# Recurrence of a gated layer: gates handled one by one, candidate and new state by scans over pairs, activation scale from a register

## The chip, the cores and the metric

The kernel runs on one core of a Trainium2 chip. The metric is the device time of one execution in microseconds (us), taken as the median over runs. In the text: PE is TensorE (matmuls; PEld its weight loads), DVE is VectorE, ACT is ScalarE, POOL is GpSimd. L12 is line 12 of the kernel's file.

## What is computed

A sandwich of two blocks on x of shape (8, 512, 128): attention in a neighbourhood of 13 tokens, then a mixture of experts whose routing comes from a recurrent layer. Each block is followed by a layer norm and a residual. The part that matters here is the recurrence, 512 steps over the sequence with a batch of 8 and a state of 1024 = 8 chunks x 128:

```python
def step(h, xw_t):
    hw = h @ gru_w_hh.T
    xr, xz, xn = jnp.split(xw_t, 3, axis=-1)
    hr, hz, hnn = jnp.split(hw, 3, axis=-1)
    r = jax.nn.sigmoid(xr + hr)
    z = jax.nn.sigmoid(xz + hz)
    n = jnp.tanh(xn + r * hnn)
    h_new = (1.0 - z) * n + z * h
    return (h_new, h_new)
_, hs = jax.lax.scan(step, h0, jnp.swapaxes(xw, 0, 1))
```

## The kernel before

The program is a row of blocks: loading and transposing weights, attention, preparing the recurrence, the recurrence, loading expert weights, routing scores and experts. The change touches the block that prepares the recurrence (from L760) and the recurrence itself (from L831). Both are written out by hand for each engine, with semaphores; nothing is scheduled by a tool, and each engine runs its list in order.

The state lies transposed: 128 partitions, and in the free dimension 8 chunks x 8 batch entries. It is cut into two halves, A and B, of 4 chunks, 32 elements for each partition. `h_parts` holds the state as two float16 parts (rounded value and remainder), which are the stationary operand of the matmuls; `h_full` holds it in float32. The steps run in pairs (q = 0 and 1), and 8 pairs make a tile of 16 steps; there are 32 tiles.

In each step PE computes the gates of both halves, in one PSUM bank each: 64 matmuls for A and 64 for B (`state_share`, L868). A's sum needs state half B as well, and the other way round. So PE waits for the new half A (`h_ready[0]`, L905), does the 32 matmuls of bank A that use it and 16 of bank B, waits for the new half B (`h_ready[1]`, L911), does the other 32 of bank A, signals `gates_ps[0]`, does the last 48 of bank B, and signals `gates_ps[1]`. Eight matmuls each of the token's share (L876) stand in between.

DVE handles first half A wholly, then half B (L979 to L984), each with three functions:

- `turn`: two transposes from PSUM to `turned`, gates r and z together (128x256, L946), then the candidate's share (128x128, L947), which frees the bank.
- `before_tanh`: adds the two float16 parts' products (L928, once for r and z, once for the candidate), waits for ACT's sigmoid over r and z (L1012, 128x64, result `rz`), multiplies r by the candidate's share (L957) and adds the token's share `xn_pair` (L959).
- `after_tanh`: waits for ACT's tanh (L1015) and for POOL, then L968 (`fresh` = tanh x (1-z)), L970 (the sum with `keep` = z x h as the first float16 part), L971 (the same sum in float32), L973 (the remainder, which sets `h_ready`).

POOL makes `keep` (L855) and `not_z` (L856) out of z. ACT gives both activations their scale as a [128, 1] operand (`scale=unscale[:, 0:1]`), and copies the new state to `history` (L1020, semaphore `kept`). After half B DVE does a share of the routing dot products (L746 and L751 for q = 0; L934, L937, L742 and L751 for q = 1). At the first pair of each tile PE, ACT and DVE also turn the tile before into routing rows (L724, L728, L733, L736).

## Time and profile before

| what | value |
|---|---|
| time, median of 3 runs | 4774.18 us (4764.96 to 4792.71) |
| profiled execution, span | 4784.5 us |
| PE, DVE, ACT, POOL busy | 83%, 69%, 25%, 16% of the span |
| recurrence | from about 577 us to about 4330 us of the span (first and last sigmoid of L1012) |
| granted TensorE clock in the recurrence | 0.99 to 1.00 of full speed |

For the profiled execution no time is given other than its span, the time from the first to the last instruction; it lies between the runs' lowest and highest time. In a timeline a row has the start, the length, the engine, the line and the operation, and in brackets how long the engine had been idle and what ended that. Rows of instructions of one line that follow each other are merged (x2, x80). VectorE starts an instruction that waits for nothing before the one ahead has ended, so the difference of two starts is what the first one costs the row.

### The profile page before, as it was taken

To read this page: it belongs to the slowest core of one execution; us is meant where nothing else is said; L and a number is where in the kernel's file an instruction comes from. 1 tells how busy PE (TensorE), PEld (TensorE's weight loads), DVE (VectorE), ACT (ScalarE), POOL (GpSimd) and SP (SyncE) were. 2 spreads that over 40 slices of the span, in tenths; PEclk is the share of its full clock that TensorE was granted. 3 is DMA by queue.
4 is the path that set the end of the run, shared out by engine and by line. 5 is a ranking of instruction groups with operands and counts; after the bars stand their busy time and mean duration, and the time that the engine had idled before them with its cause. 6 is when DMAs were issued, how large, how long until landed. Compare 5 with 4: busy or idle time off the path is not lost. (4 is left out here: it accounts for less than half of the span.)

```text
span 4784.5 us, 185112 instructions
## 1 busy us (share of the span) xinstructions
PE 3953.2 (83%) x76430; PEld 2476.3 (52%) x76430; DVE 3284.3 (69%) x13296; ACT 1204.3 (25%) x3094; POOL 768.7 (16%) x2439
## 2 busy tenths in 40 slices
PE   4998488888888888888888888888888888885999
PEld 3776354555544545544545545555554555453665
DVE  2668577777777777777777777777777777776555
ACT  1111322222222222222222222222222222222232
POOL 1111011111111111111111111111111111110000
PEclk9869799999999999999999999999999999997999
DMA  2001300000000000000000000000000000001000
GB/s 59 18 31 57 111 0 0 0 0 0 0 0 0 0 0 0 0 0 0 0 0 0 0 0 0 0 0 0 0 0 0 0 0 0 0 0 32 9 13 11
DMA packets 45745, 40.85 MB, mean 9 GB/s; under 512 B 11668, under 2 KB 39572, under 8 KB 45716
## 3 DMA queue, kind: packets, MB, share of 16 engines
q1 hardware_dynamic: 45716, 40.48, 2.7%
q8 instruction: 16, 0.26, 0.0%
q14 instruction: 13, 0.11, 0.0%
HBM read 36.28 MB, written 4.19 MB: 8 GB/s over the span
## 5 line engine op out<-in xcount | busy, mean ns | idle before, releaser
L868 PE MATMUL psum<-room,h_parts 128*32 128x384 f16 x65536 | 2904.9, 328 | 595.1 <-DVE h_parts L973 595.1
L868 PEld LDWEIGHTS psum<-room,h_parts 128*32 128x32 f16 x65536 | 1670.9, 97 | 1695.4 <-DVE h_parts L973 912.2
L1012 ACT ACTIVATE rz<-gates,unscale 128x64 f32<-128x64 f32 x1024 | 356.3, 348 | 1830.3 <-DVE gates L928 1830.3
L855 POOL TENSOR_TENSOR keep<-rz,h_full 128x32 f32<-128x32 f32 x1024 | 262.3, 256 | 2991.5 <-ACT rz L1012 2984.8
L946 DVE STREAM_TRANSPOSE turned<-psum 128x256 f32<-128x256 f32 x1024 | 454.1, 443 | 51.8 <-PE psum L868 16.9
L968 DVE TENSOR_TENSOR fresh<-n_act,not_z 128x32 f32<-128x32 f32 x1024 | 196.6, 192 | 401.7 <-ACT n_act L1015 397.4
L1015 ACT ACTIVATE n_act<-pre_n,unscale 128x32 f32<-128x32 f32 x1024 | 329.5, 322 | 497.4 <-DVE pre_n L959 497.4
L957 DVE TENSOR_TENSOR pre_n<-rz,gates 128x32 f32<-128x32 f32 x1024 | 197.2, 193 | 301.8 <-ACT rz L1012 301.8
L751 DVE TENSOR_REDUCE gram<-products 128x640 f32 (+3 forms) x528 | 327.6, 620 | 109.2 <-DVE products L742 53.8
L856 POOL TENSOR_SCALAR not_z<-rz,neg_h_scale,h_scale 128x32 f32<-128x32 f32 x1024 | 375.1, 366 | 0.0
L876 PE MATMUL psum<-w_ih_s,x_now 128*32 128x256 f16 x6152 | 305.1, 275 | 44.9 <-DVE turned L947 35.7
L928 DVE TENSOR_TENSOR gates<-turned 128x64 f32<-128x64 f32 (+1 forms) x2048 | 309.6, 187 | 0.0
L1291 PE MATMUL psum<-xn2T,room 128*128 x576 | 262.0, 600 | 38.8 <-DVE room L1366 31.4
L746 DVE TENSOR_TENSOR products<-routes 128x640 f32 (+1 forms) x264 | 218.0, 826 | 101.2 <-ACT routes L736 100.6
L947 DVE STREAM_TRANSPOSE turned<-psum 128x128 f32<-128x128 f32 x1024 | 280.1, 274 | 0.0
L1020 ACT COPY history<-h_parts 128x128 f16 (+1 forms) x512 | 152.6, 298 | 459.8 <-DVE h_parts L973 459.8
L876 PEld LDWEIGHTS psum<-w_ih_s,x_now 128*32 128x32 f16 x6152 | 160.0, 98 | 162.1 <-DVE turned L947 48.1
L959 DVE TENSOR_TENSOR pre_n<-pre_n,xn_pair 128x32 f32<-128x32 f32 x1024 | 196.7, 192 | 34.9
L973 DVE TENSOR_TENSOR h_parts<-h_full,h_parts 128x32 f16<-128x32 f32 x1024 | 196.2, 192 | 35.6
L970 DVE TENSOR_TENSOR h_parts<-fresh,keep 128x32 f16<-128x32 f32 x1024 | 196.5, 192 | 34.9
L1366 DVE TENSOR_TENSOR room<-room,psum 128x512 f32<-128x512 f32 x144 | 98.1, 686 | 142.9 <-ACT room L1308 140.9
L971 DVE TENSOR_TENSOR h_full<-fresh,keep 128x32 f32<-128x32 f32 x1024 | 188.4, 184 | 0.0
(151 smaller groups left out, 2725.6 us busy)
## 6 DMA issues: line engine op xcount, KB each, us to landing
xs_room<-in_L_ffn_gru_w_hh_dram SPq DMA_DIRECT2D x16, 1536.0 KB, 6.2
room<-in_L_attn_x_dram SPq DMA_DIRECT2D x8, 256.0 KB, 5.4
x_scratch<-room SPq DMA_DIRECT2D x8, 256.0 KB, 2.3
room<-x_scratch SPq DMA_DIRECT2D x32, 64.0 KB, 2.2
out_dram<-room SPq DMA_DIRECT2D x32, 64.0 KB, 2.0
xs_room<-in_L_ffn_gru_w_ih_dram SPq DMA_DIRECT2D x3, 512.0 KB, 5.1
xs_room<-in_L_ffn_gate_w_dram SPq DMA_DIRECT2D x2, 512.0 KB, 4.6
xs_room<-in_L_ffn_up_w_dram SPq DMA_DIRECT2D x2, 512.0 KB, 3.9
```

The costliest lines, as they stand in the source:

```text
L746: return nc.vector.tensor_tensor(products[:, :, :], routes[:, 0, bass.ds(e, 1), :].to_broadcast([P, NSHIFT, P]), routes[:, 0, bass.ds(e, N ...
L751: return nc.vector.tensor_reduce(dst, products[:, 0:n, :], axis=AX_X, op=ALU.add)
L855: nc.gpsimd.tensor_tensor(keep[:, half, :], rz[:, half, 1, :], h_full[:, q, half * HB:(half + 1) * HB], ALU.mult)
L856: nc.gpsimd.tensor_scalar(not_z[:, half, :], rz[:, half, 1, :], neg_h_scale[:, 0:1], h_scale_f[:, 0:1], ALU.mult, ALU.add).then_inc(keep_d ...
L868: last = nc.tensor.matmul(psum[32 * j:32 * j + 32, half, 0:3 * P], h_parts[:, q, c, :], w_hh_s[:, s, half, 4 * c + j, :, :].rearrange("p g ...
L876: last = nc.tensor.matmul(psum[32 * j:32 * j + 32, columns, 0:2 * P], x_now[:, :], w_ih_s[:, s, j, place:place + 2, :].rearrange("p g r -> ...
L928: return nc.vector.tensor_tensor(by_chunk(gates[:, half, g:g + n, :].rearrange("p g k -> p (g k)")), by_part[:, :, 2 * q, :], by_part[:, : ...
L946: nc.vector.transpose(turned[:, half, 0:2, :], bank[:, 0:2, :]).then_inc(rz_turned[half], 1)
L947: nc.vector.transpose(turned[:, half, 2:3, :], bank[:, 2:3, :]).then_inc(bank_free[half], 1)
L1012: nc.scalar.activation(rz[:, half, :, :], gates[:, half, 0:2, :], ACT.Sigmoid, scale=unscale[:, 0:1]).then_inc(rz_done[half], 1)
L1015: nc.scalar.activation(n_act[:, half, :], pre_n[:, half, 1, :], ACT.Tanh, scale=unscale[:, 0:1]).then_inc(n_done[half], 1)
L1291: last = nc.tensor.matmul(psum[:, 2 * (u % RING) + k, :], expT[:, e, FC * k + f, :], toks, start=True, stop=True)
```

## The change

It rewrites what DVE, ACT and POOL do in a step, and leaves PE's list as it is.

- r, z and the candidate's share are transposed and summed one by one (`to_gates`): three transposes of 128x128 and three sums of 128x32, where two transposes and two sums stood. ACT has a sigmoid for r and one for z, each of 128x32.
- The product and sum ahead of the tanh become one scan (`tensor_tensor_scan` with multiply and add) over 64 elements in which pairs stand side by side: `r_pairs` = (0, r) and `hx_pairs` = (candidate's share, token's share). The scan's running value at the first element of a pair is 0 x old + share, and at the second r x share + token's share. The new state comes from a second scan over `z_pairs` = (0, not_z) and `nk_pairs` = (tanh, keep). The results are read from every second element.
- The state in float32 lies in `h_pairs`, at every second element. Its first float16 part is a copy of it (L977) instead of a sum of its own.
- `not_z` moves from POOL to DVE; POOL keeps the product z x h.
- ACT takes the scale from a register that is loaded once ahead of the loops, and the function table for sigmoid is loaded there too.
- DVE's wait for `kept` moves from the transposes of half A to its second scan.
- POOL clears `r_pairs` and `z_pairs` in the preparing block.

```diff
@@ -664,18 +664,17 @@
         h_parts = sb("h_parts", [P, 2, CH, 4 * B], F16)
         x_now = sb("x_now", [P, 4 * B], F16)
-        h_full = sb("h_full", [P, 2, CH * B])
+        h_pairs = sb("h_pairs", [P, 2, CH * B, 2])
         turned = sb("turned", [P, 2, 3, P])
-        gates = sb("gates", [P, 2, 3, HB])
+        gates = sb("gates", [P, 2, 2, HB])
         xn_turned = sb("xn_turned", [P, 2 * P])
-        xn_pair = sb("xn_pair", [P, CH, 2, B])
+        hx_pairs = sb("hx_pairs", [P, 2, CH * B, 2])
         neg_h_scale = sb("neg_h_scale", [P, 1])
-        rz = sb("rz", [P, 2, 2, HB])
-        pre_n = sb("pre_n", [P, 2, 2, HB])
-        n_act = sb("n_act", [P, 2, HB])
-        keep = sb("keep", [P, 2, HB])
-        not_z = sb("not_z", [P, 2, HB])
-        fresh = sb("fresh", [P, 2, HB])
+        r_pairs = sb("r_pairs", [P, 2, HB, 2])
+        z_act = sb("z_act", [P, 2, HB])
+        pre_n = sb("pre_n", [P, 2, HB, 2])
+        z_pairs = sb("z_pairs", [P, 2, HB, 2])
+        nk_pairs = sb("nk_pairs", [P, 2, HB, 2])
         x_mean = sb("x_mean", [P, B])
         history = sb("history", [P, CH, 2, SP_T, B], F16)
         ident_16 = sb("ident_16", [P, P], F16)
...
@@ -765,6 +765,8 @@
                 nc.gpsimd.memset(x_parts[:, L, :], 0.0)
                 nc.gpsimd.memset(history[:, :, :, :, :], 0.0)
                 nc.gpsimd.memset(x_tile[:, :], 0.0)
+                nc.gpsimd.memset(r_pairs[:, :, :, :], 0.0)
+                nc.gpsimd.memset(z_pairs[:, :, :, :], 0.0)
                 nc.gpsimd.tensor_copy(ident_16[:, :], ident[:, :])
                 pool.wait_ge(h0_top, 1)
                 nc.gpsimd.partition_all_reduce(h_all[:, :], w_top[:, :], P, RMAX).then_inc(h0_all, 1)
...
@@ -851,9 +854,9 @@
                     nc.gpsimd.tensor_copy(x_now[:, :].rearrange("p (t k) -> p t k", t=2), x_parts[:, bass.ds(t0 + 2, 2), :]).then_inc(x_staged, 1)
                     for q in range(2):
                         for half in range(2):
-                            pool.wait_ge(rz_done[half], t0 + q + 1)
-                            nc.gpsimd.tensor_tensor(keep[:, half, :], rz[:, half, 1, :], h_full[:, q, half * HB:(half + 1) * HB], ALU.mult)
-                            nc.gpsimd.tensor_scalar(not_z[:, half, :], rz[:, half, 1, :], neg_h_scale[:, 0:1], h_scale_f[:, 0:1], ALU.mult, ALU.add).then_inc(keep_done[half], 1)
+                            pool.wait_ge(z_done[half], t0 + q + 1)
+                            nc.gpsimd.tensor_tensor(nk_pairs[:, half, :, 1], z_act[:, half, :], h_pairs[:, q, half * HB:(half + 1) * HB, 1],
+                                                    ALU.mult).then_inc(keep_done[half], 1)
                     if first:
                         nc.gpsimd.tensor_copy(x_tile[:, :], xn2T[:, bass.ds(n * P, P)]).then_inc(tile_staged, 1)
@@ -922,11 +925,9 @@
             @block.vector
             def _(dve):
-                def summed(q, half, g, n):
-                    by_part = turned[:, half, g:g + n, :].rearrange("p g (k s b) -> p (g k) s b", s=4, b=B)
-                    return nc.vector.tensor_tensor(by_chunk(gates[:, half, g:g + n, :].rearrange("p g k -> p (g k)")),
-                                                   by_part[:, :, 2 * q, :], by_part[:, :, 2 * q + 1, :], ALU.add)
+                def summed(q, half, g, dst):
+                    by_part = turned[:, half, g, :].rearrange("p (k s b) -> p k s b", s=4, b=B)
+                    return nc.vector.tensor_tensor(by_chunk(dst), by_part[:, :, 2 * q, :], by_part[:, :, 2 * q + 1, :], ALU.add)
                 def turn_xn(pairs):
@@ -934,41 +935,46 @@
                     nc.vector.transpose(xn_turned[:, :], psum[:, XN_BANK, 0:2 * P]).then_inc(xn_read, 1)
                     dve.wait_ge(xn_read, pairs)
                     by_part = xn_turned[:, :].rearrange("p (k q s b) -> p k q s b", q=2, s=2, b=B)
-                    nc.vector.tensor_tensor(xn_pair[:, :, :, :], by_part[:, :, :, 0, :], by_part[:, :, :, 1, :],
-                                            ALU.add).then_inc(xn_ready, 1)
-                def turn(t1, q, half):
+                    nc.vector.tensor_tensor(hx_pairs[:, :, :, 1].rearrange("p q (c b) -> p c q b", b=B),
+                                            by_part[:, :, :, 0, :], by_part[:, :, :, 1, :], ALU.add).then_inc(xn_ready, 1)
+                def to_gates(t1, q, half):
                     bank = psum[:, half, 0:3 * P].rearrange("p (g r) -> p g r", g=3)
                     dve.wait_ge(gates_ps[half], t1)
+                    nc.vector.transpose(turned[:, half, 0, :], bank[:, 0, :]).then_inc(r_turned[half], 1)
+                    nc.vector.transpose(turned[:, half, 1, :], bank[:, 1, :]).then_inc(z_turned[half], 1)
+                    dve.wait_ge(r_turned[half], t1)
+                    summed(q, half, 0, gates[:, half, 0, :]).then_inc(r_in[half], 1)
+                    nc.vector.transpose(turned[:, half, 2, :], bank[:, 2, :]).then_inc(bank_free[half], 1)
+                    dve.wait_ge(z_turned[half], t1)
+                    summed(q, half, 1, gates[:, half, 1, :]).then_inc(z_in[half], 1)
+                    dve.wait_ge(bank_free[half], t1 + 1)
+                    summed(q, half, 2, hx_pairs[:, q, half * HB:(half + 1) * HB, 0]).then_inc(n_in[half], 1)
+                def row(pairs):
+                    return pairs.rearrange("p k two -> p (k two)")
+                def to_state(t1, q, half):
+                    here = slice(half * HB, (half + 1) * HB)
+                    dve.wait_ge(n_in[half], t1)
+                    dve.wait_ge(r_done[half], t1)
+                    nc.vector.tensor_tensor_scan(row(pre_n[:, half, :, :]), row(r_pairs[:, half, :, :]), row(hx_pairs[:, q, here, :]),
+                                                 0.0, ALU.mult, ALU.add).then_inc(pre_done[half], 1)
+                    dve.wait_ge(z_done[half], t1)
+                    nc.vector.tensor_scalar(z_pairs[:, half, :, 1], z_act[:, half, :], neg_h_scale[:, 0:1], h_scale_f[:, 0:1],
+                                            ALU.mult, ALU.add).then_inc(not_z_done[half], 1)
                     if half == 0:
                         dve.wait_ge(kept, t1)
-                    nc.vector.transpose(turned[:, half, 0:2, :], bank[:, 0:2, :]).then_inc(rz_turned[half], 1)
-                    nc.vector.transpose(turned[:, half, 2:3, :], bank[:, 2:3, :]).then_inc(bank_free[half], 1)
-                def before_tanh(t1, q, half):
-                    dve.wait_ge(rz_turned[half], t1)
-                    summed(q, half, 0, 2).then_inc(gates_in[half], 1)
-                    dve.wait_ge(bank_free[half], t1 + 1)
-                    summed(q, half, 2, 1).then_inc(n_in[half], 1)
-                    dve.wait_ge(rz_done[half], t1)
-                    dve.wait_ge(n_in[half], t1)
-                    nc.vector.tensor_tensor(pre_n[:, half, 0, :], rz[:, half, 0, :], gates[:, half, 2, :], ALU.mult).then_inc(hn_scaled[half], 1)
-                    dve.wait_ge(hn_scaled[half], t1)
-                    nc.vector.tensor_tensor(by_chunk(pre_n[:, half, 1, :]), by_chunk(pre_n[:, half, 0, :]),
-                                            xn_pair[:, half * HALF:(half + 1) * HALF, q, :], ALU.add).then_inc(pre_done[half], 1)
-                def after_tanh(t1, q, half):
+                    parts = h_parts[:, 1 - q, half * HALF:(half + 1) * HALF, :]
+                    full = h_pairs[:, 1 - q, here, 1]
+                    dve.wait_ge(not_z_done[half], t1)
+                    dve.wait_ge(keep_done[half], t1)
                     dve.wait_ge(n_done[half], t1)
-                    dve.wait_ge(keep_done[half], t1)
-                    full = h_full[:, 1 - q, half * HB:(half + 1) * HB]
-                    parts = h_parts[:, 1 - q, half * HALF:(half + 1) * HALF, :]
-                    nc.vector.tensor_tensor(fresh[:, half, :], n_act[:, half, :], not_z[:, half, :], ALU.mult).then_inc(fresh_done[half], 1)
-                    dve.wait_ge(fresh_done[half], t1)
-                    nc.vector.tensor_tensor(part(parts, 2 * (1 - q)), by_chunk(fresh[:, half, :]), by_chunk(keep[:, half, :]), ALU.add)
-                    nc.vector.tensor_tensor(full, fresh[:, half, :], keep[:, half, :], ALU.add).then_inc(first_part[half], 1)
+                    nc.vector.tensor_tensor_scan(row(h_pairs[:, 1 - q, here, :]), row(z_pairs[:, half, :, :]), row(nk_pairs[:, half, :, :]),
+                                                 0.0, ALU.mult, ALU.add).then_inc(full_done[half], 1)
+                    dve.wait_ge(full_done[half], t1)
+                    nc.vector.tensor_copy(part(parts, 2 * (1 - q)), by_chunk(full)).then_inc(first_part[half], 1)
                     dve.wait_ge(first_part[half], t1)
                     nc.vector.tensor_tensor(part(parts, 2 * (1 - q) + 1), by_chunk(full), part(parts, 2 * (1 - q)), ALU.subtract).then_inc(h_ready[half], 1)
@@ -976,12 +982,10 @@
                     t0 = n * SP_T + 2 * i
                     for q in range(2):
                         t1 = t0 + q + 1
-                        turn(t1, q, 0)
-                        before_tanh(t1, q, 0)
-                        after_tanh(t1, q, 0)
-                        turn(t1, q, 1)
-                        before_tanh(t1, q, 1)
-                        after_tanh(t1, q, 1)
+                        to_gates(t1, q, 0)
+                        to_state(t1, q, 0)
+                        to_gates(t1, q, 1)
+                        to_state(t1, q, 1)
                         if q == 0:
@@ -1003,17 +1007,24 @@
             @block.scalar
             def _(act):
+                by_unscale = nc.scalar.alloc_register("by_unscale")
+                nc.scalar.reg_load(by_unscale, unscale[0:1, 0:1].bitcast(U32))
+                nc.scalar.preload_act_table(ACT.Sigmoid)
                 def pair(n, i, first):
                     t0 = n * SP_T + 2 * i
                     for q in range(2):
                         t1 = t0 + q + 1
                         for half in range(2):
-                            act.wait_ge(gates_in[half], t1)
-                            nc.scalar.activation(rz[:, half, :, :], gates[:, half, 0:2, :], ACT.Sigmoid,
-                                                 scale=unscale[:, 0:1]).then_inc(rz_done[half], 1)
+                            act.wait_ge(r_in[half], t1)
+                            nc.scalar.activation(r_pairs[:, half, :, 1], gates[:, half, 0, :], ACT.Sigmoid,
+                                                 scale=by_unscale).then_inc(r_done[half], 1)
+                            act.wait_ge(z_in[half], t1)
+                            nc.scalar.activation(z_act[:, half, :], gates[:, half, 1, :], ACT.Sigmoid,
+                                                 scale=by_unscale).then_inc(z_done[half], 1)
                             act.wait_ge(pre_done[half], t1)
-                            nc.scalar.activation(n_act[:, half, :], pre_n[:, half, 1, :], ACT.Tanh,
-                                                 scale=unscale[:, 0:1]).then_inc(n_done[half], 1)
+                            nc.scalar.activation(nk_pairs[:, half, :, 0], pre_n[:, half, :, 1], ACT.Tanh,
+                                                 scale=by_unscale).then_inc(n_done[half], 1)
                         act.wait_ge(h_ready[1], t1 + 1)
                         act.wait_ge(tile_ps, n + 1)
```

How the lists of instructions move, at two places. DVE, half A of a step at q = 0, before (A and B at a semaphore's end are the halves):

```order
L946 STREAM_TRANSPOSE turned<-psum 128x256 [waits kept,gates_psA]
L947 STREAM_TRANSPOSE turned<-psum 128x128
L928 TENSOR_TENSOR gates<-turned 128x64 [waits rz_turnedA]
L952 REGISTER_ALU
L928 TENSOR_TENSOR gates<-turned 128x32 [waits bank_freeA]
L957 TENSOR_TENSOR pre_n<-rz,gates 128x32 [waits n_inA,rz_doneA]
L959 TENSOR_TENSOR pre_n<-pre_n,xn_pair 128x32 [waits hn_scaledA]
L968 TENSOR_TENSOR fresh<-n_act,not_z 128x32 [waits keep_doneA,n_doneA]
L970 TENSOR_TENSOR h_parts<-fresh,keep 128x4x8 [waits fresh_doneA]
L971 TENSOR_TENSOR h_full<-fresh,keep 128x32
L973 TENSOR_TENSOR h_parts<-h_full,h_parts 128x4x8 [waits first_partA]
```

and after the change:

```order
L945 STREAM_TRANSPOSE turned<-psum 128x128 [waits gates_psA]
L946 STREAM_TRANSPOSE turned<-psum 128x128
L930 TENSOR_TENSOR gates<-turned 128x32 [waits r_turnedA]
L949 STREAM_TRANSPOSE turned<-psum 128x128
L930 TENSOR_TENSOR gates<-turned 128x32 [waits z_turnedA]
L952 REGISTER_ALU
L930 TENSOR_TENSOR hx_pairs<-turned 128x32 [waits bank_freeA]
L962 SCALAR_TENSOR_TENSOR pre_n<-r_pairs,hx_pairs 128x64 [waits r_doneA,n_inA]
L965 TENSOR_SCALAR z_pairs<-z_act,neg_h_scale,h_scale 128x32 [waits z_doneA]
L974 SCALAR_TENSOR_TENSOR h_pairs<-z_pairs,nk_pairs 128x64 [waits keep_doneA,n_doneA,not_z_doneA,kept]
L977 CAST h_parts<-h_pairs 128x4x8 [waits full_doneA]
L979 TENSOR_TENSOR h_parts<-h_pairs,h_parts 128x4x8 [waits first_partA]
```

Ten instructions and a register operation have become eleven and a register operation. The two scans are printed as SCALAR_TENSOR_TENSOR of 128x64; the second one has four waits, `kept` among them, and L965 stands ahead of it.

ACT, the entry to the loops and half A of the first step, before:

```order
L838 UNCONDITIONAL_BRANCH
L838 ISA
L1012 ACT_TABLE_LOAD
L1012 ACTIVATE rz<-gates,unscale 128x64 [waits gates_inA]
L1015 ACTIVATE n_act<-pre_n,unscale 128x32 [waits pre_doneA]
```

and after:

```order
L1011 TENSOR_LOAD unscale
L1012 ACT_TABLE_LOAD
L841 UNCONDITIONAL_BRANCH
L841 ISA
L1020 ACTIVATE r_pairs<-gates 128x32 [waits r_inA]
L1023 ACTIVATE z_act<-gates 128x32 [waits z_inA]
L1026 ACTIVATE nk_pairs<-pre_n 128x32 [waits pre_doneA]
```

The table load stood inside the loop over tiles (the branch at L838 opens it) and now stands ahead of it (L841 opens it); one activation has become two.

## Rows read from the trace of the kernel before

**Rows 1.** The page: busy time and share of the span of each engine.
```profile
PE 3953.2 (83%) x76430; PEld 2476.3 (52%) x76430; DVE 3284.3 (69%) x13296; ACT 1204.3 (25%) x3094; POOL 768.7 (16%) x2439
```

**Rows 2.** Timeline, steady recurrence: start us, length us, engine, line, operation, count, [idle before].
```profile
2403.19 3.43 PE L868 MATMUL psum<-room,h_parts 128*32 128x384 f16 x80 [0.50 <-DVE h_parts L973]
...
2404.84 0.44 DVE L946 STREAM_TRANSPOSE turned<-psum 128x256 f32<-128x256 f32 x1
2405.21 0.28 DVE L947 STREAM_TRANSPOSE turned<-psum 128x128 f32<-128x128 f32 x1
2405.41 0.30 DVE L928 TENSOR_TENSOR gates<-turned 128x64 f32<-128x64 f32 x2
2405.62 0.35 ACT L1012 ACTIVATE rz<-gates,unscale 128x64 f32<-128x64 f32 x1 [2.07 <-DVE gates L928]
2406.00 0.19 DVE L957 TENSOR_TENSOR pre_n<-rz,gates 128x32 f32<-128x32 f32 x1 [0.30 <-ACT rz L1012]
2406.05 0.26 POOL L855 TENSOR_TENSOR keep<-rz,h_full 128x32 f32<-128x32 f32 x1 [3.81 <-ACT rz L1012]
2406.23 0.19 DVE L959 TENSOR_TENSOR pre_n<-pre_n,xn_pair 128x32 f32<-128x32 f32 x1
...
2406.30 0.37 POOL L856 TENSOR_SCALAR not_z<-rz,neg_h_scale,h_scale 128x32 f32<-128x32 f32 x1
...
2406.46 0.32 ACT L1015 ACTIVATE n_act<-pre_n,unscale 128x32 f32<-128x32 f32 x1 [0.49 <-DVE pre_n L959]
2406.81 0.19 DVE L968 TENSOR_TENSOR fresh<-n_act,not_z 128x32 f32<-128x32 f32 x1 [0.39 <-ACT n_act L1015]
2407.04 0.19 DVE L970 TENSOR_TENSOR h_parts<-fresh,keep 128x32 f16<-128x32 f32 x1
...
2407.37 0.19 DVE L973 TENSOR_TENSOR h_parts<-h_full,h_parts 128x32 f16<-128x32 f32 x1
2407.48 0.44 DVE L946 STREAM_TRANSPOSE turned<-psum 128x256 f32<-128x256 f32 x1
...
2407.61 1.48 PE L868 MATMUL psum<-room,h_parts 128*32 128x384 f16 x32 [0.77 <-DVE h_parts L973]
...
2410.24 3.05 PEld L868 LDWEIGHTS psum<-room,h_parts 128*32 128x32 f16 x80 [0.67 <-DVE h_parts L973]
2410.24 3.44 PE L868 MATMUL psum<-room,h_parts 128*32 128x384 f16 x80 [0.28 <-DVE h_parts L973]
...
2419.05 0.44 DVE L946 STREAM_TRANSPOSE turned<-psum 128x256 f32<-128x256 f32 x1
```

**Rows 3.** Timeline around the start of a new tile of 16 steps.
```profile
2453.38 1.28 ACT L1012 ACT_TABLE_LOAD   x1 [0.15 <-issue]
...
2455.57 0.35 ACT L1012 ACTIVATE rz<-gates,unscale 128x64 f32<-128x64 f32 x1 [0.91 <-DVE gates L928]
...
2473.13 0.45 DVE L946 STREAM_TRANSPOSE turned<-psum 128x256 f32<-128x256 f32 x1 [1.14 <-PE psum L868]
```

**Rows 4.** Groups by line and shape, VectorE: count | busy us, mean ns | idle before.
```profile
L937 DVE TENSOR_TENSOR xn_pair<-xn_turned 128x128 f32<-128x128 f32 x257 | 75.2, 293 | 8.8
...
L1142 DVE TENSOR_TENSOR room<-room 128x256 f32<-128x256 f32 x21 | 8.9, 425 | 2.0 <-issue 0.4
L1338 DVE TENSOR_SCALAR room<-room,mv,rstd 128x128 f32<-128x128 f32 x32 | 8.9, 342 | 0.7
...
L393 DVE RECIPROCAL total<-total 128x64 f32<-128x64 f32 x8 | 4.4, 553 | 0.6
...
L1142 DVE TENSOR_TENSOR room<-gram,room 128x256 f32<-128x256 f32 x5 | 3.1, 613 | 0.4
```

**Rows 5.** Groups by line and shape, ScalarE.
```profile
L733 ACT ACTIVATE routes<-psum,h_unscale 128x512 f32<-128x512 f32 x99 | 60.6, 682 | 7.0 <-PE psum L728 7.0
...
L736 ACT COPY routes<-psum 128x512 f32<-128x512 f32 x66 | 35.6, 603 | 0.0
...
L1130 ACT ACTIVATE room<-room 128x32 f32<-128x32 f32 x1 | 0.3, 260 | 15.6 <-DVEq L1207 15.6
```

14 lines of the change are left out of this document (8 added, 6 removed).

## The prediction

> **What bounds the kernel now.** I read the page first. PE is busy for 83% of the span and DVE for 69% [rows 1], so the page alone suggests PE. The page's own chain of waits doesn't help, because it covers only the end of the program. The timeline of the steady recurrence does [rows 2]. Two steps take 2419.05 - 2404.84 = 14.21 us, one step 7.1 us, and 512 steps are some 3640 of the 4784.5 us. Within a step DVE works on half A from the transpose at 2404.84 to that of half B at 2407.48, 2.64 us, then as long on half B. The other 1.8 us are PE's first 32 matmuls with the new half B, up to the next transpose. While DVE is on a half, PE comes to a stop: 0.77 us ahead of the matmuls at 2407.61, 0.67 us by its weight loads ahead of those at 2410.24 (0.28 us by the modelled ends of its matmuls), 0.50 us at 2403.19 [rows 2]. So a step ends by the chain DVE, ACT, DVE, ACT, DVE of two halves, one after the other. Each 0.1 us off a half is 1024 x 0.1 = 102 us off the kernel, as long as PE's stops last.
>
> The half in full, as starts from its first transpose [rows 2]: transpose of r and z 0; transpose of the candidate 0.37; sum of r and z 0.57; ACT's sigmoid 0.78; product 1.16; sum 1.39; tanh 1.62; fresh 1.97; first part 2.20; remainder 2.53; next transpose 2.64. From these come the prices I use. An instruction of 32 elements costs 0.22 us if the next one needs its result (0.19 long and 0.03 to be seen), and 0.11 us if not (two in a row take 0.30, the last of them 0.19). A transpose of 128 elements costs the next one 0.20 us and is 0.28 long. ACT starts 0.21 us after a sum starts; DVE starts 0.03 us after ACT ends, POOL 0.08 us.
>
> **The change, part by part.** *Three transposes and three sums.* Transpose r 0, transpose z 0.20, sum r 0.40, transpose of the candidate 0.51, sum z 0.71. The candidate's sum waits for its transpose (0.51 + 0.28 + 0.03) and starts at 0.82. ACT starts r at 0.61 and has it by about 0.90 even if it is as long as the 0.32 of today's 32-element activation. So ACT no longer ends this wait: DVE's own sums do, and the next instruction can start at 0.82 + 0.22 = 1.04, where the product started at 1.16. One more instruction stands in DVE's row, and 0.12 us are won, because the sigmoid now lies beside DVE's work.
>
> *Elements at every second place.* The candidate's sum now writes so, and the copy and the remainder at the end read so. No row has such a step. At no cost the lower end; for the upper the sum at L1142, which takes 425 ns with its elements side by side and 613 ns where it reads `gram`, whose elements lie 10 apart: 188/256 = 0.73 ns for each element, 0.024 us for 32 [rows 4]. I take the upper end, as its row is the only one, and the price is small: 3 x 0.024 = 0.07 us a half. The scans themselves read and write side by side.
>
> *The scans.* The trace has no scan. Below: 64 elements are in and out in 0.19 us, as a plain instruction of that kind. Above: the reciprocal at L393, whose 64 elements go round for several cycles each, 553 ns [rows 4]. A scan's element needs the one before it through a multiply and an add, so 64 elements are 128 dependent operations, and I take the 128-element sum at L937, 293 ns [rows 4]. Then the first scan costs 0.29 + 0.04 up to the tanh, where product and sum cost 0.46 (1.16 to 1.62): 0.13 us won. The second costs 0.32, and the copy after it 0.22; that replaces fresh 0.22, first part 0.11 and full state 0.22 (1.97 to 2.53, 0.56): 0.02 us won. The Trainium skill (DVE: opcode table, Datapath and trigger behaviour) says of the built-in scan that it runs at half throughput, which is the same two cycles for an element. No run here shows it yet.
>
> *The scale from a register.* ACT's activation from PSUM with a [128, 1] scale takes 682 ns for 512 elements, its copy without one 603 ns [rows 5]: 0.08 us for the operand. Taken off today's 0.32 of the tanh this leaves 0.24 us. A 32-element activation with no such operand stands at 260 ns [rows 5], though with its elements four apart. Ends: no gain at all (a register might be read as late as an operand), and 0.09 us. I take 0.08. The Trainium skill (ScalarE: Activation LUTs, What ACT_TABLE_LOAD costs) gives about 93 ns for each such operand; the sum would be 13 us lower by it.
>
> *z, not_z and keep.* ACT starts z at 0.92, and has it at 1.17. POOL's product starts at 1.25 and is there by 1.55. On DVE not_z stands behind the first scan; it starts at about 1.27 and, with two [128, 1] operands, takes some 0.25: L1338, the same with 128 elements, takes 342 ns, less 96 elements at about 1 ns (425 - 293 ns for 128 more) [rows 4]. It is there by 1.55. Both cost nothing as long as the tanh ends later, which it does at about 1.66. The cover is 0.1 us.
>
> *The table load.* 32 loads of 1.28 us go. The one at 2453.38 ends at 2454.66, and ACT then idles another 0.91 us until DVE's sum releases it at 2455.57 [rows 3]: nothing won. The Trainium skill (ScalarE: Activation LUTs, same section) adds a drain of about 1.38 us to each load. That would end at 2456.04, behind the start that the row shows, so the trace disagrees, and I go by the row. The wait for `kept` is for a copy of 0.3 us made in the step before; it had ended at either place.
>
> **Sum.** A half before 2.64 us. Won 0.12 + 0.13 + 0.02 + 0.08 = 0.35, given back 0.07 (and 0.01 of rounding): 0.27 us. Times 1024 = 276 us. Right after a tile's start PE runs late, and DVE waits 1.14 us for it at 2473.13 [rows 3]. That half's gain is lost in at most 32 tiles, 32 x 0.27 = 9 us; I take half, 4 us. PE's stops are 0.28 us and more, so it stays behind DVE elsewhere. 4784.5 - 272 = 4512 for the profiled execution. That lies 10 us over the median of the runs, so the median becomes **4502 us**.
>
> **The rivals.** *POOL or not_z ends last (20%).* DVE's scan and POOL's product meet at 1.04 to 1.55, and not_z runs against POOL's product. If POOL's product could start only when not_z has ended (1.52 + 0.26 + 0.05), the second scan would start at 1.83 instead of 1.66, 0.17 us late. They may overlap in part, so I price 0.12 us: 1024 x 0.12 = 123 more, 4625 us. Against it: today L959 starts at 2406.23 inside POOL's L855 (2406.05 for 0.26) and is 0.19 long, as L968 is with POOL idle [rows 2]. The Trainium skill (SBUF — State Buffer, Who interferes with whom) has it that a DVE instruction with two inputs from SBUF, or in a 2-port mode as `tensor_scalar` can be, and a POOL one that reads SBUF block each other wholly. L959's row doesn't agree.
>
> *The register is no better than the operand (8%).* [...] 0.08 x 1024 = 82 more, 4584 us.
>
> *A scan as cheap as a plain instruction (12%).* Each is 0.10 us shorter. The first counts in full; the second scan's start then meets POOL's 1.55, so about 0.18 in all: 4502 - 184 = 4318 us. For it speaks only that nothing in the trace excludes it.
>
> *A slow scan (5%), the case of the other side.* If an element has to leave the whole pipeline before the next may enter, the scan is nearer L393's 553 ns. Both scans then add 0.26: a half is 0.52 - 0.27 = 0.25 us longer than before, 4774 + 256 = 5030 us. It decides from 0.293 + 0.27/2 = 0.43 us for one scan.
>
> **How the numbers follow.** The forecast has 55%, and its own range is 4420 (steps of two free, 0.07, and 0.01 more from the register) to 4560. With the rivals at 4584 and 4625 it reaches 4640. Below I go to 4390, and leave out most of the cheap scan (12%) and the slow one (5%). A difference of 0.5% (24 us) is about what a measurement can tell from none. Faster: all but the slow scan and a small rest, 0.93; same 0.02; slower 0.05.
>
> **What would show it.** Right: two scans of about 290 ns, sigmoid and tanh of about 240 ns, DVE's wait ahead of the first scan gone, the wait ahead of the second one ended by ACT's tanh, a half of 2.37 us, two steps of about 13.1 us, PE's stops shorter by 0.27 us each, and POOL busy for some 370 us less. Wrong: the second scan released by POOL or by not_z (first rival), activations of 32 elements still at 320 ns (second), scans under 230 or over 430 ns (third and fourth), or stops of PE that have gone, with DVE's transposes waiting for matmuls.

## The result and the profile after

| kernel | median (lowest to highest) | ratio to before [95%] |
|---|---|---|
| before, on the same chip | 4770.83 us (4764.96 to 4792.71) | 1 |
| after | 4520.57 us (4519.59 to 4525.81) | 0.946 [0.9432, 0.9487] |

The change makes the kernel 5.4% faster. The time lies in the range, 19 us over the forecast.

The page of the kernel after, span and busy time (against [rows 1]):
```profile
span 4519.1 us, 186108 instructions
...
PE 3925.9 (87%) x76430; PEld 2455.3 (54%) x76430; DVE 3548.1 (79%) x14320; ACT 1190.9 (26%) x4087; POOL 405.6 (9%) x1417
```
Groups by line and shape of the same kernel (count | busy us, mean ns | idle before, and what ended it):
```profile
L871 PE MATMUL psum<-room,h_parts 128*32 128x384 f16 x65536 | 2892.5, 327 | 364.7 <-DVE h_parts L979 349.6
...
L974 DVE TENSOR_TENSOR_SCAN h_pairs<-z_pairs,nk_pairs 128x64 f32<-128x64 f32 x1024 | 299.0, 292 | 210.3 <-ACT nk_pairs L1026 205.8 <-POOL nk_pairs L858 4.5
...
L945 DVE STREAM_TRANSPOSE turned<-psum 128x128 f32<-128x128 f32 x1024 | 317.9, 310 | 26.6 <-issue 7.8 <-PE psum L871 6.9
...
L962 DVE TENSOR_TENSOR_SCAN pre_n<-r_pairs,hx_pairs 128x64 f32<-128x64 f32 x1024 | 298.7, 292 | 34.9
```
VectorE is busy for 264 us more than before, and the kernel is 250 us shorter. What went is waiting: ahead of the first scan only 34.9 us remain, and no ScalarE ends them. Ahead of the second scan there are 210.3. PE's matmuls of the recurrence are busy for 2892 us, and were for 2905 before; their idle time fell from 595 to 365 us.

The timeline of the kernel after, half A of a step in the steady recurrence (against [rows 2]; start, length, engine, line, operation, [idle before]):
```profile
2400.25 0.32 DVE L945 STREAM_TRANSPOSE turned<-psum 128x128 f32<-128x128 f32 x1
2400.49 0.27 DVE L946 STREAM_TRANSPOSE turned<-psum 128x128 f32<-128x128 f32 x1
2400.69 0.15 DVE L930 TENSOR_TENSOR gates<-turned 128x32 f32<-128x32 f32 x1
2400.76 0.30 DVE L949 STREAM_TRANSPOSE turned<-psum 128x128 f32<-128x128 f32 x1
2400.87 0.23 ACT L1020 ACTIVATE r_pairs<-gates 128x32 f32<-128x32 f32 x1 [1.92 <-DVE gates L930]
2400.99 0.15 DVE L930 TENSOR_TENSOR gates<-turned 128x32 f32<-128x32 f32 x1
2401.10 0.20 DVE L930 TENSOR_TENSOR hx_pairs<-turned 128x32 f32<-128x32 f32 x1
2401.18 0.23 ACT L1023 ACTIVATE z_act<-gates 128x32 f32<-128x32 f32 x1
2401.33 0.29 DVE L962 TENSOR_TENSOR_SCAN pre_n<-r_pairs,hx_pairs 128x64 f32<-128x64 f32 x1
2401.48 0.26 POOL L858 TENSOR_TENSOR nk_pairs<-z_act,h_pairs 128x32 f32<-128x32 f32 x1 [3.11 <-ACT z_act L1023]
2401.54 0.28 DVE L965 TENSOR_SCALAR z_pairs<-z_act,neg_h_scale,h_scale 128x32 f32<-128x32 f32 x1
2401.66 0.23 ACT L1026 ACTIVATE nk_pairs<-pre_n 128x32 f32<-128x32 f32 x1 [0.25 <-DVE pre_n L962]
...
2402.02 0.29 DVE L974 TENSOR_TENSOR_SCAN h_pairs<-z_pairs,nk_pairs 128x64 f32<-128x64 f32 x1 [0.20 <-ACT nk_pairs L1026]
2402.35 0.18 DVE L977 CAST h_parts<-h_pairs 128x32 f16<-128x32 f32 x1
2402.56 0.19 DVE L979 TENSOR_TENSOR h_parts<-h_pairs,h_parts 128x32 f16<-128x32 f32 x1
2402.67 0.31 DVE L945 STREAM_TRANSPOSE turned<-psum 128x128 f32<-128x128 f32 x1
...
2413.49 0.32 DVE L945 STREAM_TRANSPOSE turned<-psum 128x128 f32<-128x128 f32 x1
```
A half takes 2402.67 - 2400.25 = 2.42 us (2.64 before), two steps 2413.49 - 2400.25 = 13.24 us (14.21 before). One place doesn't fit the prediction: the tanh ends at 2401.66 + 0.23 = 2401.89, and the second scan starts at 2402.02, 0.13 us later. In [rows 2] the instruction behind the tanh, L968, follows it by 0.03 us (2406.46 + 0.32, then 2406.81).

The part before the recurrence varies from run to run: in the profiles of this case the first sigmoid starts between 532 and 577 us. To compare two profiles I therefore use the **stretch**: from the first to the last start of the r sigmoid, the 1024 halves alone. One line's instructions, in the kernel before, then after (duration min/median/max, first and last start):
```profile
L1012 ACT ACTIVATE rz<-gates,unscale x1024: 347/348/351, 577.3 to 4326.4; 128x64 f32<-128x64 f32 x171
```
```profile
L1020 ACT ACTIVATE r_pairs<-gates x1024: 231/233/237, 563.7 to 4061.7; 128x32 f32<-128x32 f32 x171
```
3749.1 us became 3498.0, 251.1 less. The halves explain 1024 x 0.22 = 225 us. The other 26 are taken up below.

Where a **median** is named below, it is taken over the 512 halves A (or B) of a profile, in us from the half's first transpose. By it the second scan of half A starts at 1.757, and the next half 2.408 us after this one; the single half above reads 1.77 and 2.42.

### The profile page after: what moved, and what is told of

It reads as the page before. It is cut to its first block and busy times, and to the rows that moved or that the text cites. A ratio compares the mean times of both kernels' runs of the same rounds, so it can differ in the third digit from the quotient of the medians.

```text
span 4519.1 us, 186108 instructions
## 1 busy us (share of the span) xinstructions
PE 3925.9 (87%) x76430; PEld 2455.3 (54%) x76430; DVE 3548.1 (79%) x14320; ACT 1190.9 (26%) x4087; POOL 405.6 (9%) x1417
## 5 line engine op out<-in xcount | busy, mean ns | idle before, releaser
L1020 ACT ACTIVATE r_pairs<-gates 128x32 f32<-128x32 f32 x1024 | 238.8, 233 | 1725.3 <-DVE gates L930 1725.3
L858 POOL TENSOR_TENSOR nk_pairs<-z_act,h_pairs 128x32 f32<-128x32 f32 x1024 | 260.7, 255 | 3022.2 <-ACT z_act L1023 3014.9
L974 DVE TENSOR_TENSOR_SCAN h_pairs<-z_pairs,nk_pairs 128x64 f32<-128x64 f32 x1024 | 299.0, 292 | 210.3 <-ACT nk_pairs L1026 205.8
L751 DVE TENSOR_REDUCE gram<-products 128x640 f32 (+3 forms) x528 | 327.5, 620 | 113.2 <-DVE products L746 57.8
L945 DVE STREAM_TRANSPOSE turned<-psum 128x128 f32<-128x128 f32 x1024 | 317.9, 310 | 26.6 <-issue 7.8
L962 DVE TENSOR_TENSOR_SCAN pre_n<-r_pairs,hx_pairs 128x64 f32<-128x64 f32 x1024 | 298.7, 292 | 34.9
L949 DVE STREAM_TRANSPOSE turned<-psum 128x128 f32<-128x128 f32 x1024 | 313.1, 306 | 0.0
L930 DVE TENSOR_TENSOR gates<-turned 128x32 f32<-128x32 f32 x2048 | 307.5, 150 | 0.0
L1026 ACT ACTIVATE nk_pairs<-pre_n 128x32 f32<-128x32 f32 x1024 | 238.0, 232 | 255.9 <-DVE pre_n L962 255.9
L965 DVE TENSOR_SCALAR z_pairs<-z_act,neg_h_scale,h_scale 128x32 f32<-128x32 f32 x1024 | 284.8, 278 | 0.0
L946 DVE STREAM_TRANSPOSE turned<-psum 128x128 f32<-128x128 f32 x1024 | 280.7, 274 | 0.0
L1023 ACT ACTIVATE z_act<-gates 128x32 f32<-128x32 f32 x1024 | 235.0, 229 | 68.4
L979 DVE TENSOR_TENSOR h_parts<-h_pairs,h_parts 128x32 f16<-128x32 f32 x1024 | 197.0, 192 | 35.4
L977 DVE CAST h_parts<-h_pairs 128x32 f16<-128x32 f32 x1024 | 186.8, 182 | 34.9
```

What stands on the lines that cost most here:

```text
L751: return nc.vector.tensor_reduce(dst, products[:, 0:n, :], axis=AX_X, op=ALU.add)
L858: nc.gpsimd.tensor_tensor(nk_pairs[:, half, :, 1], z_act[:, half, :], h_pairs[:, q, half * HB:(half + 1) * HB, 1], ALU.mult).then_inc(keep ...
L930: return nc.vector.tensor_tensor(by_chunk(dst), by_part[:, :, 2 * q, :], by_part[:, :, 2 * q + 1, :], ALU.add)
L945: nc.vector.transpose(turned[:, half, 0, :], bank[:, 0, :]).then_inc(r_turned[half], 1)
L946: nc.vector.transpose(turned[:, half, 1, :], bank[:, 1, :]).then_inc(z_turned[half], 1)
L949: nc.vector.transpose(turned[:, half, 2, :], bank[:, 2, :]).then_inc(bank_free[half], 1)
```

## Experiments

All are edits of the kernel after. Their times compare with its 4520.57 us, their stretches with its 3498.0. The kernel before ran beside each set of runs, with medians between 4766 and 4777 us; the ratios are to those.

**Where 0.10 us ahead of the second scan comes from.** An instruction of VectorE carries one wait; the program as built puts the others ahead of it in instructions that do nothing but wait, two semaphores to each. Which ones are left to the scan depends on the order in the code. Read from the built programs, "|" between instructions, an entry without a name being an instruction that only waits:
```
                 half A                                        half B
before  L968     keep | L968: n_done                           the same
after   L974     keep | n_done, not_z | scan: kept             n_done, keep | scan: not_z
a1               not_z | keep, kept | scan: n_done             keep, not_z | scan: n_done
a2               not_z | keep, n_done | scan: kept             keep, not_z | scan: n_done
b1               keep, not_z | scan: n_done                    the same
c1               keep | r_done, not_z | scan: n_done           the same
```
*a1*, the wait for the tanh put on the scan in both halves:
```diff
+                    dve.wait_ge(n_done[half], t1)
                     if half == 0:
                         dve.wait_ge(kept, t1)
...
                     dve.wait_ge(keep_done[half], t1)
-                    dve.wait_ge(n_done[half], t1)
```


> The change as it is, with the four waits ahead of the second scan (tanh, not_z, keep, kept) written in another order, so that the wait for the tanh, which comes last, stands on the scan instruction itself in both halves and no longer in a wait instruction ahead of it. In the changed kernel the scan starts 0.13 us after the tanh has ended, where fresh (before) started 0.03 us after it. Theory D (a last wait in an instruction of its own costs DVE some 0.10 us): the gap falls to 0.03 us, a half lasts 2.32 us instead of 2.42, 1024 x 0.10 = 102 us less than 4520, about 4418 us. Rival S (ACT's result at every second place is there later than its row shows): the gap stays 0.13, 4520 us. Rival C (not_z or POOL's product ends last): not_z is there 0.03 us ahead of the tanh, so the gap would fall by 0.03 at most, 4490 us.

*a2*, the same line behind the wait for `kept`, which puts it on the scan in half B alone:
```diff
                         dve.wait_ge(kept, t1)
...
+                    dve.wait_ge(n_done[half], t1)
                     dve.wait_ge(not_z_done[half], t1)
                     dve.wait_ge(keep_done[half], t1)
-                    dve.wait_ge(n_done[half], t1)
```

> The same change of order, but one that puts the wait for the tanh on the scan in half B alone; in half A kept stays on it and the wait for the tanh in an instruction of its own. Theory D: the gap is 0.03 us in half B and 0.13 in half A, 512 x 0.10 = 51 us less, about 4469 us. Rivals S and C: both halves alike, 4520 or 4490 us.

Measured: a1 4474.48 us (4439.01 to 4503.52), 0.94 [0.935, 0.9451], stretch 3445.3, where about 4418 us were expected; a2 4472.48 us (4437.19 to 4487.93), 0.9396 [0.9353, 0.9439], stretch 3446.3, as expected. The timeline of a1, half B, then half A:
```profile
2401.55 0.28 DVE L965 TENSOR_SCALAR z_pairs<-z_act,neg_h_scale,h_scale 128x32 f32<-128x32 f32 x1
2401.67 0.23 ACT L1026 ACTIVATE nk_pairs<-pre_n 128x32 f32<-128x32 f32 x1 [0.25 <-DVE pre_n L962]
2401.93 0.29 DVE L974 TENSOR_TENSOR_SCAN h_pairs<-z_pairs,nk_pairs 128x64 f32<-128x64 f32 x1
...
2405.65 0.28 DVE L965 TENSOR_SCALAR z_pairs<-z_act,neg_h_scale,h_scale 128x32 f32<-128x32 f32 x1
2405.77 0.23 ACT L1026 ACTIVATE nk_pairs<-pre_n 128x32 f32<-128x32 f32 x1 [0.25 <-DVE pre_n L962]
2406.13 0.29 DVE L974 TENSOR_TENSOR_SCAN h_pairs<-z_pairs,nk_pairs 128x64 f32<-128x64 f32 x1 [0.20 <-ACT nk_pairs L1026]
```
Half B's scan starts 0.03 us behind the tanh, and 512 x 0.10 = 51 us are gone from the stretch. Half A's gap is still 0.13 us, though its scan now carries the wait for the tanh: the theory fell in this form. There `not_z`, ready only at 2405.93, is held by the first of two waiting instructions, and the scan starts 0.20 us after it. In half B one such instruction stands between, and the scan starts 0.10 us after `not_z` (2401.83 to 2401.93). So it isn't the tanh's wait as such. The reading is now this: each instruction that only waits passes its semaphore on some 0.1 us late, the delays of several in a row add up, and the scan starts when the latest of these chains has ended. Two runs tell this from a cost that goes by the number of waits.

*b1*: `kept` goes ahead of the first scan, so that half A too needs only one waiting instruction and the scan carries the tanh's wait.
```diff
+                    if half == 0:
+                        dve.wait_ge(kept, t1)
                     nc.vector.tensor_tensor_scan(row(pre_n[:, half, :, :]), ...
...
-                    if half == 0:
-                        dve.wait_ge(kept, t1)
+                    dve.wait_ge(n_done[half], t1)
...
-                    dve.wait_ge(n_done[half], t1)
```


> As the run that put the wait for the tanh on the second scan, but half A's wait for kept (done long before) moved ahead of the first scan, so that both halves have the same three waits ahead of the second scan: one wait instruction with POOL's product and not_z, and the tanh on the scan. There half A kept its gap of 0.13 us, with two wait instructions behind the semaphore of not_z, and half B came down to 0.03. Theory D2 (each wait instruction takes DVE's queue some 0.07 to 0.10 us from its release to the next instruction, and what counts is how many stand behind the last semaphore or shortly before it): half A comes down to 0.03 too, 512 x 0.10 = 51 us less than that run in the stretch of the recurrence (3445 to about 3394 us from first to last sigmoid), about 4420 us. Rival A (half A's scan is held by something else that only half A has, such as PE's reads): half A keeps 0.13, stretch 3445 us, about 4472 us.

*c1*: b1 with a second waiting instruction (`r_done`, there long before, is waited for again). POOL's product is then held by the first of the two, `not_z` by the second:
```diff
                     dve.wait_ge(keep_done[half], t1)
+                    dve.wait_ge(r_done[half], t1)
```

> The run with kept moved early (4418 us, stretch from first to last sigmoid 3391 us, gap of 0.03 us ahead of the second scan in both halves), with one wait more ahead of the second scan, for a semaphore that is set long before (the sigmoid of r). The built program then has two wait instructions there: the first for POOL's product (there at about 1.54 us of the half), the second for not_z (about 1.60) and the added one, and the tanh on the scan. Theory D2 (what costs is how many instructions stand behind the semaphore that comes last or nearly last): only the scan stands behind not_z, as in the run it starts from, so nothing changes: 4418 us, stretch 3391, gap 0.03 to 0.05. Theory D3 (every second wait instruction costs 0.10 us, wherever its semaphore comes): gap 0.13, stretch 3391 + 102 = 3493 us, 4520 us.

Measured: **b1 4418.39 us** (4390.0 to 4430.96), 0.9239 [0.9175, 0.9303], stretch 3390.8; c1 4420.15 us (4414.31 to 4428.26), 0.9254 [0.9204, 0.9304], stretch 3406.3. The timeline of b1, half A, and the next half's start:
```profile
2401.84 0.32 DVE L945 STREAM_TRANSPOSE turned<-psum 128x128 f32<-128x128 f32 x1
...
2403.25 0.23 ACT L1026 ACTIVATE nk_pairs<-pre_n 128x32 f32<-128x32 f32 x1 [0.25 <-DVE pre_n L964]
2403.51 0.29 DVE L974 TENSOR_TENSOR_SCAN h_pairs<-z_pairs,nk_pairs 128x64 f32<-128x64 f32 x1
2404.16 0.31 DVE L945 STREAM_TRANSPOSE turned<-psum 128x128 f32<-128x128 f32 x1
```
The gap is 0.03 us in both halves, a half is 2.32 us, and the stretch is 107 us shorter: 1024 x 0.10 = 102, and 5 that the reading of a half doesn't resolve (0.01 us of a half is 10 us). In c1 the extra instruction costs 15.5 us in 1024 halves, 0.015 us each, not 0.10; a cost for each waiting instruction is out. The timeline of c1:
```profile
2406.48 0.25 POOL L858 TENSOR_TENSOR nk_pairs<-z_act,h_pairs 128x32 f32<-128x32 f32 x1 [3.05 <-ACT z_act L1024]
...
2406.65 0.23 ACT L1027 ACTIVATE nk_pairs<-pre_n 128x32 f32<-128x32 f32 x1 [0.25 <-DVE pre_n L964]
2406.93 0.29 DVE L975 TENSOR_TENSOR_SCAN h_pairs<-z_pairs,nk_pairs 128x64 f32<-128x64 f32 x1
```
The scan starts 0.05 us behind the tanh and 0.20 behind the end of POOL's product (2406.73), which has two waiting instructions ahead of it, as `not_z` has in a1's half A; by the medians it is 1.478 to 1.678 here and 1.555 to 1.756 there. So the 0.015 us are not the price of a wait for something that is long there. By this reading POOL's product, there 0.15 us ahead of the tanh, has become the chain that ends last.

*c3*, the wait for `kept` put back ahead of the transposes, where the kernel before has it:
```diff
                     dve.wait_ge(gates_ps[half], t1)
+                    if half == 0:
+                        dve.wait_ge(kept, t1)
                     nc.vector.transpose(turned[:, half, 0, :], ...
...
-                    if half == 0:
-                        dve.wait_ge(kept, t1)
```

> The change with DVE's wait for kept back ahead of the transposes of half A. Before, half A's first transpose came 1.74 us after PE had started on the new half B at q = 1, in the changed kernel 1.67. Theory K (the wait instruction for kept is what took the 0.06 us, once in two steps): 256 x 0.06 = 15 us more there, stretch 3498 to 3513; and nothing gained at the second scan, whose last wait still stands in an instruction of its own. Rival M (that 0.06 came from the three-way transposes or PE): stretch 3498.

4544.03 us (4531.42 to 4557.95), 0.9517 [0.9461, 0.9574], stretch 3521.5, 23.5 longer. From half B's first transpose to that of the next step's half A it takes 4.28 us where a new pair of steps begins, 4.21 in the kernel after: 0.07 x 256 = 18 us. The other steps are as before. The copy isn't what VectorE waits for there:
```profile
2411.10 0.30 ACT L1031 COPY history<-h_parts 128x128 f16 x1 [1.00 <-DVE h_parts L979]
2412.21 0.42 DVE L751 TENSOR_REDUCE gram<-products 128x256 f32 x1 [0.21 <-DVE products L742]
2412.76 0.32 DVE L947 STREAM_TRANSPOSE turned<-psum 128x128 f32<-128x128 f32 x1
```
It ended at 2411.40, 1.36 us ahead of the transpose, and VectorE is idle for 0.13 us ahead of it (0.06 in the kernel after). So a wait whose semaphore is long there costs 0.07 us at this place, behind the turn of the loop. In the other steps the transpose starts before L751 has ended, and it costs nothing. VectorE also waits 15.2 us for matmuls, where the kernel after has 6.9. Together that is 26 us, against 23.5 measured. The kernel before has both: in every second step it takes 4.51 us for 4.43 (medians), and its waits for matmuls are 16.9 us. So 225 + 18 + 10 = 253 us account for the 251.1 of the stretch.

The gap ahead of the second scan is 0.13 us in c3 too: with `kept` gone from there, the built program has `n_done`, `keep` | scan: `not_z` in both halves. So it wasn't `kept` that pushed the tanh's wait off the scan, but the new wait for `not_z` and the order of the lines. `kept` adds the second waiting instruction of half A, and that counts once the tanh's wait is on the scan (a1 against b1, 54 us).

**What each part of the change is worth.**

*a3*, the scale as a [128, 1] operand again in the three activations:
```diff
-                                                 scale=by_unscale).then_inc(r_done[half], 1)
+                                                 scale=unscale[:, 0:1]).then_inc(r_done[half], 1)
```

> The change with the three activations taking their scale from the [128, 1] operand again. Theory: each activation is 0.09 us longer (232 to about 322 ns); of these only the tanh is on the path, because r would end at 0.97 us of the half and the first scan starts at 1.08. 1024 x 0.09 = 92 us more than 4520, about 4612 us. Rival R (the register is worth nothing, 32 elements without a second half are what made them short): 4520 us.

4630.4 us (4616.1 to 4646.53), 0.9708 [0.9659, 0.9758], stretch 3606.0. Its groups:
```profile
L1024 ACT ACTIVATE nk_pairs<-pre_n,unscale 128x32 f32<-128x32 f32 x1024 | 333.7, 326 | 162.6 <-DVE pre_n L962 162.6
...
L965 DVE TENSOR_SCALAR z_pairs<-z_act,neg_h_scale,h_scale 128x32 f32<-128x32 f32 x1024 | 336.6, 329 | 0.0
```
326 ns against 232: the register is worth 0.09 us in each activation, and 108 us in all, because only the tanh lies on the path (1024 x 0.094 = 96), and VectorE's waits for matmuls are 18.5 us for 6.9. The Trainium skill (ScalarE: Activation LUTs, What ACT_TABLE_LOAD costs) gives about 93 ns for such an operand; the trace agrees with 94. `not_z` takes 329 ns, with POOL's product starting after it, and 278 in the kernel after, where POOL starts first.

*a4*, r and z transposed, summed and activated together again, 64 elements each (both gates in one tensor of pairs, POOL and L965 waiting for `r_done`):
```diff
-                    nc.vector.transpose(turned[:, half, 0, :], bank[:, 0, :]).then_inc(r_turned[half], 1)
-                    nc.vector.transpose(turned[:, half, 1, :], bank[:, 1, :]).then_inc(z_turned[half], 1)
+                    nc.vector.transpose(turned[:, half, 0:2, :], bank[:, 0:2, :]).then_inc(r_turned[half], 1)
```


> The change with r and z transposed, summed and activated together again (two transposes, two sums, one sigmoid of 64 elements), everything else as in the change, the wait for the sigmoid standing on the first scan. Theory P (taking the gates apart won only because it put a 0.35 us sigmoid beside DVE's sums; with the register the sigmoid of 64 elements is about 0.26 us): sigmoid from 0.78 to 1.04, first scan at 1.07 against 1.08 in the change, so nothing is lost: 4510 us, within 20. Rival G (taking them apart is a gain of its own of 0.12 us a half): 1024 x 0.1 = 100 us more, 4620 us.

4518.86 us (4502.12 to 4527.4), 0.9479 [0.9436, 0.9522], stretch 3504.0: no difference. With the scale in a register the 64-element sigmoid takes 263 ns, so it is done soon after the candidate's sum. Its groups, ScalarE and VectorE:
```profile
L1017 ACT ACTIVATE rz_pairs<-gates 128x64 f32<-128x64 f32 x1024 | 269.7, 263 | 1892.5 <-DVE gates L931 1892.5
...
L960 DVE TENSOR_TENSOR_SCAN pre_n<-rz_pairs,hx_pairs 128x64 f32<-128x64 f32 x1024 | 298.8, 292 | 213.2 <-ACT rz_pairs L1017 213.2
```
The first scan waits 213 us for ScalarE again, 0.21 us a half, but VectorE has one transpose and one sum fewer to do. With the scale in a register, gates one by one only trade waiting for work.

*b2*, the first scan undone (product, a wait for it, sum, on the same pairs):
```diff
-                    nc.vector.tensor_tensor_scan(row(pre_n[:, half, :, :]), ...
+                    nc.vector.tensor_tensor(pre_n[:, half, :, 0], r_pairs[:, half, :, 1], hx_pairs[:, q, here, 0], ALU.mult).then_inc(hn_scaled[half], 1)
+                    dve.wait_ge(hn_scaled[half], t1)
+                    nc.vector.tensor_tensor(pre_n[:, half, :, 1], pre_n[:, half, :, 0], hx_pairs[:, q, here, 1], ALU.add).then_inc(pre_done[half], 1)
```


> The change with the first scan taken back to a product and a sum over every second element, all else as in the change. Theory: product and sum cost 0.22 + 0.23 us up to the tanh, the scan 0.33; 0.12 us more a half, 1024 x 0.12 = 123 us, stretch 3498 to about 3621, 4643 us. Rival T (a scan's two cycles for an element are worth no more than the two instructions, as not_z behind it or the sums ahead of it set the tanh): 4520 us.

4718.37 us (4711.51 to 4731.73), 0.9878 [0.9819, 0.9936], stretch 3688.8, 191 longer where 123 were expected. The two instructions:
```profile
L964 DVE TENSOR_TENSOR pre_n<-pre_n,hx_pairs 128x32 f32<-128x32 f32 x1024 | 232.2, 227 | 34.9
...
L962 DVE TENSOR_TENSOR pre_n<-r_pairs,hx_pairs 128x32 f32<-128x32 f32 x1024 | 198.8, 194 | 34.9
```
A half is 0.165 us longer by the medians (2.575 for 2.408 in half A): 169 us. Waits for matmuls are 32.7 us, 26 more; together 195, against 191 measured. The sum is 227 ns long (192 before). That isn't the step of its operands alone, as the product ahead of it, L962, has all of its own at every second place too and takes 194. POOL's product runs beside the sum here; which of the causes left it is, no run shows. Without these 35 ns the first scan is worth 0.13 us a half.

*b3*, the second scan undone (`fresh`, first part and full state one by one, on the pairs):
```diff
-                    nc.vector.tensor_tensor_scan(row(h_pairs[:, 1 - q, here, :]), ...
+                    nc.vector.tensor_tensor(fresh[:, half, :], nk_pairs[:, half, :, 0], z_pairs[:, half, :, 1], ALU.mult).then_inc(full_done[half], 1)
...
-                    nc.vector.tensor_copy(part(parts, 2 * (1 - q)), by_chunk(full)).then_inc(first_part[half], 1)
+                    nc.vector.tensor_tensor(part(parts, 2 * (1 - q)), by_chunk(fresh[:, half, :]), by_chunk(nk_pairs[:, half, :, 1]), ALU.add)
+                    nc.vector.tensor_tensor(full, fresh[:, half, :], nk_pairs[:, half, :, 1], ALU.add).then_inc(first_part[half], 1)
```

> The change with the second scan and the copy taken back to product, first part, full state (fresh, then two sums), all else as in the change. Theory: from its start to the next transpose the scan with copy and remainder takes 0.33 + 0.21 + 0.11 = 0.65 us, the old way 0.22 + 0.33 + 0.11 = 0.66; 10 us more, stretch 3498 to about 3508, 4530 us, no difference to be measured. Rival U (the second scan is worth as much as the first): 123 us more, 4643 us.

4527.68 us (4524.97 to 4539.48), 0.9483 [0.9429, 0.9538]; stretch 3516.2, 18.2 longer, of which 8 are waits for matmuls (14.8 us for 6.9). The second scan is worth some 10 us by itself, which the runs' times don't tell from nothing.

*b4*, `not_z` computed on POOL behind its product, as in the kernel before:
```diff
-                                                    ALU.mult).then_inc(keep_done[half], 1)
+                                                    ALU.mult)
+                            nc.gpsimd.tensor_scalar(z_pairs[:, half, :, 1], z_act[:, half, :], ...).then_inc(keep_done[half], 1)
```


> The change with not_z on POOL again, behind its product, all else as in the change. Theory: POOL starts at 1.23 us of the half, its product and not_z take 0.25 + 0.37 us, seen by DVE at about 1.92, where the second scan now starts at 1.77; in half A, where that wait stands in an instruction of its own, at 2.02. On average 0.20 us more a half, 1024 x 0.20 = 205 us, 4725 us (between 4670 and 4780). It would show that moving not_z to DVE is what lets the shorter chain count. Rival N (POOL is hidden anyway): 4520 us, or a little less, as DVE has one instruction fewer.

4673.26 us (4663.86 to 4686.81), 0.9787 [0.973, 0.9845], stretch 3658.8, 161 longer. Its timeline, half B, then half A:
```profile
2401.15 0.37 POOL L860 TENSOR_SCALAR z_pairs<-z_act,neg_h_scale,h_scale 128x32 f32<-128x32 f32 x1
...
2401.55 0.34 DVE L972 TENSOR_TENSOR_SCAN h_pairs<-z_pairs,nk_pairs 128x64 f32<-128x64 f32 x1 [0.51 <-POOL z_pairs L860]
...
2405.40 0.37 POOL L860 TENSOR_SCALAR z_pairs<-z_act,neg_h_scale,h_scale 128x32 f32<-128x32 f32 x1
2405.86 0.29 DVE L972 TENSOR_TENSOR_SCAN h_pairs<-z_pairs,nk_pairs 128x64 f32<-128x64 f32 x1 [0.57 <-POOL z_pairs L860]
```
POOL ends last once `not_z` is its work. In half B its wait stands on the scan, which starts 0.03 us behind it; in half A it stands in a waiting instruction, and the scan starts 0.09 behind it. By the medians its start moves by 0.113 us in half B and 0.172 in half A: 512 x 0.285 = 146 us, and 18.6 more of waits for matmuls (25.5 for 6.9), 165 against 161 measured. In the kernel before the tanh came late enough to hide it (0.37 us ended at 2406.67, the tanh at 2406.78 [rows 2]). With `not_z` on POOL 90 of the 251 us are left: moving it to VectorE is what lets the scans and the register pay in full.

*c2*, no table load ahead of the loop:
```diff
-                nc.scalar.preload_act_table(ACT.Sigmoid)
```

> The change without the load of the function table ahead of the loops; the built program then loads it at the start of each of the 32 tiles, as before. Theory: the load (1.28 us) ends well before the first sum of r releases the sigmoid, since ACT idles 1.9 us there; nothing changes, 4520 us, stretch 3498. Rival L (load and a drain behind it, 2.66 us together, against 1.9 us of idle time): 0.7 us for each of 32 tiles, 24 us more, stretch 3522.

4498.66 us (4491.53 to 4533.66), 0.9447 [0.9384, 0.951], stretch 3498.2 against 3498.0. ScalarE's group:
```profile
L1019 ACT ACT_TABLE_LOAD x32 | 41.1, 1283 | 8.3 <-issue 4.8 <-PEq L760 3.5
```
32 loads are back, and the stretch is the same to 0.2 us. The loads were free, and the 22 us by which the median is lower lie outside the recurrence: its first sigmoid starts at 534 us, and at 564 in the kernel after. No other line of the loop loads a table, so each of these loads brings back the table that is already there; what a load of another one would cost, no run shows.

Undone one at a time, the parts cost 191 (first scan), 161 (`not_z`), 108 (register), 18 (second scan) and 6 us (gates apart) of the stretch, 484 in all, where the whole change won 251. Each is what the part is worth with the others in place, and they aren't shares of a sum.

## Why the prediction was right

The forecast of 4502 us missed by 19, and the mechanism was the one named: a half went from 2.64 to 2.42 us, where 2.37 was forecast. That the time came so close is in part luck, as the last two bullets tell. Part by part, in starts from the first transpose:

| step of the sum | forecast | measured | effect |
|---|---|---|---|
| first scan starts | 1.04, +0.02 for its stepped operand | 1.08 | +0.02 |
| scan, to the tanh | 0.33 | 0.33 | 0 |
| tanh | 0.24 | 0.23 | -0.01 |
| tanh to the second scan | 0.03 | 0.13 | +0.10 |
| scan, copy, remainder, to the next transpose | 0.65, +0.05 for stepped operands | 0.65 | -0.05 |
| the half | 2.37 | 2.42 | +0.05 (rounded) |

- **The scan.** 293 ns was taken from the 128-element sum, 292 measured. The rivals of a cheap and of a slow scan are out. Of the half throughput that the Trainium skill states (DVE: opcode table, Datapath and trigger behaviour): by this row, 64 elements cost what 128 do in a plain instruction, and the trace agrees, at this one size. The price of the first scan (0.13) was right; b2 gives 0.165, with the slower sum's 0.035 in it. The second was forecast at 0.02 and is about 0.01 (b3).
- **Elements at every second place.** The 0.07 us given back was wrong: its term came from elements 10 apart (L1142), and the sum is 193 ns, the copy 182 and the remainder 192, as plain ones are. No run shows a cost of the step: b2's product has all operands so and takes 194 ns. Its sum takes 227, for a reason that stays open.
- **Gates apart.** The 0.12 us won was reached less 0.04: a 128-element transpose behind another kind of instruction is 306 to 310 ns long, not 274, and the candidate's sum waits for it. But a4 shows that the split itself wins nothing once the register is there: the register alone would have brought it.
- **Register.** 0.08 was forecast, 0.094 measured (a3). The rival "no better than the operand" is out.
- **POOL or not_z ends last.** In the kernel after the tanh ends last, as forecast. `not_z` is there 0.07 us ahead of it (2401.82 against 2401.89), not 0.1: in a1's half A it does count. Of the Trainium skill's rule of a whole block (SBUF — State Buffer, Who interferes with whom): the first scan, with two inputs from SBUF, runs from 2401.33 to 2401.62 and POOL's product from 2401.48 to 2401.74, and both are as long as elsewhere (0.29 and 0.26 us), so the trace doesn't agree. In a3 POOL's product starts 0.09 us later, with less of the scan beside it, and is as long (255 ns). L965 and the product overlap too; where L965 starts ahead of the product it is 51 ns longer (a3).
- **The step that failed** is the one the prediction gave no term, "DVE starts 0.03 us after ACT ends": it was read where the wait stood on the working instruction, L968, and the change moved the wait into an instruction of its own. The second scan starts 0.13 us after the tanh instead; 0.10 x 1024 = 102 us, shown by b1. The text named `kept` as free at either place; c3 shows that at its old place it costs 18 us or more, and a1 against b1 that at its new one it can cost another 54.
- **What hid it.** The stretch lost 26 us beyond the halves, 18 from `kept` and some 10 from waits for matmuls, where the sum had a loss of 4: without them the kernel would be at about 4547. And 0.05 us a half had been charged for stepped operands and was not spent.
- **PE and tile starts.** 4 us of loss were taken; instead 10 were won, because the waits of [rows 3]'s kind are gone: the kernel before has 11 of them, 12.5 us, the kernel after none (below). PE's idle time fell by 230 us rather than by 276. Its four stops of two steps are 0.28, 0.50, 0.77 and 0.86 us before and 0.06, 0.27, 0.54 and 0.57 after (medians), so by the modelled ends one is nearly gone. But VectorE's transposes wait for matmuls in the first steps alone, so PE isn't the bound yet.

## What to carry to other kernels

Put the wait for the semaphore that comes last where the built program leaves it on the instruction that does the work, and take the others out of that place, to where the engine is still at work; two waiting instructions held even a semaphore back that came 0.15 us early (c1). Here two moved lines were worth 107 us, as much as the register. Read a start-to-start price from a row whose waits are built as they will be after the change. Before an operation is split so that another engine starts earlier, ask whether shortening that engine's own instruction isn't enough.

## What the runs showed of the hardware

- An instruction of VectorE that only waits passes its semaphore on late. With one between, VectorE's next instruction starts 0.13 us behind ScalarE's end (0.03 with the wait on the instruction itself), and 0.09 behind POOL's (0.03; b4). With two between it is 0.20 us, behind VectorE's own `not_z` (a1, half A) and behind POOL's product (c1). One whose semaphore had been there for over a microsecond cost 0.07 us behind the turn of the loop, and nothing where VectorE was still at work (c3).
- When the granted clock of TensorE drops, VectorE waits for matmuls. Kernel before, windows (length, busy time of PE, its weight loads, VectorE, ScalarE and POOL, then PE's clock as a share of full speed, 0.50 being 1.2 GHz, and DMA):
```profile
2464.30:2467.70 3.40, 0.69 (x16) 0.12 (x8) 2.62 (x12) 0.67 (x2) 0.61 (x2) 1.00 0.00 0
2467.70:2469.20 1.50, 1.46 (x28) 0.89 (x32) 1.16 (x6) 0.35 (x1) 0.39 (x2) 0.78 0.00 0
2469.20:2471.00 1.80, 1.80 (x32) 1.09 (x28) 1.32 (x7) 0.62 (x2) 0.67 (x3) 0.50 0.00 0
```
PE was busy 0.69 of 3.4 us, and the clock fell behind that; the wait of 1.14 us at 2473.13 [rows 3] follows. VectorE's waits for matmuls ahead of a half's first transpose (us in all, times, longest) in the kernel before and in b2, and for the kernel after (us, times):
```profile
DVE turned L946 <- PE psum L868: 16.9, 12, 4.4
```
```profile
DVE turned L945 <- PE psum L871: 32.7, 26, 4.2
```
```profile
  PE psum L871: 6.9, 2
```
One or two of them are at the start of the recurrence, in every run. The others stand at the third step of a tile: 11 before (every third tile), none after, none in b1 and c1, 25 in b2. In each of the 13 profiles there are as many as stretches of half clock between the recurrence's third step and its last. What spares the kernel after at the same place stays open.
